# A bidirectional Mamba-2 block: an unread negation taken out, one semaphore dropped, and the engines' orders rearranged

## What is computed

```python
def reference(x, ...):
    xn = layernorm(x)
    f = mamba2(xn, forward weights)
    r = flip(mamba2(flip(xn), backward weights))
    x = x + concat(f, r) @ Wo + bo
    return x + layernorm(x) @ W.T + b + (layernorm(x) @ V_r) @ C.T

def mamba2(x, ...):
    z, xBC, dt = split(x @ Win)
    xs, B, C = split(silu(causal_conv(xBC, width 4) + convb))
    dt = softplus(dt + dtb); dA = exp(dt * A)
    h = dA[t] * h + dt[t] * B[t] * xs[t];  y[t] = C[t] @ h      # 8 heads of 64, state of 64
    y = (y + D * xs) * silu(z)
    return rmsnorm(y) * normw @ Wout
```

## Time and profile before

| | us |
|---|---|
| median of 3 runs | 636.88 |
| lowest and highest | 635.69, 637.50 |
| the profiled execution, its own time | 635.01 |
| its span, first to last instruction | 633.20 |
| TensorE busy (matmuls) | 602.9, 95% |
| ScalarE busy | 545.8, 86% |
| VectorE busy | 510.0, 81% |
| GpSimd busy | 363.1, 57% |
| granted TensorE clock, mean | 0.997 of full speed |

### The profile page before, as it was taken

One profiled execution on the slowest core, in us unless ns is written; L12 is line 12 of the kernel. 1 busy time (PEld: TensorE's weight loads), 2 busy tenths in 40 slices (PEclk: granted clock), 3 DMA queues, 4 the chain that ended last, 5 costly groups with the idle time before them and its releaser, 6 DMA issues.

```text
span 633.2 us, 13301 instructions
## 1 busy us (share of the span) xinstructions
PE 602.9 (95%) x3996; PEld 492.4 (78%) x3996; DVE 510.0 (81%) x1056; ACT 545.8 (86%) x1220; POOL 363.1 (57%) x367
## 2 busy tenths in 40 slices
PE   2998999999999999999999999999999999999995
PEld 1676788887888878887888878888788878888784
DVE  3779788986979689797888869798797978788663
ACT  4799998979997998979989799889989799897862
POOL 1026656666575664765556675656647665465933
PEclk9999999999999999999999999999999999999998
DMA  7552614245160632407132361505416071332600
GB/s 223 158 180 92 208 23 132 57 119 192 25 184 0 193 116 65 144 9 248 51 126 83 98 211 25 182 3 177 131 29 180 1 217 59 101 111 67 211 1 33
DMA packets 43544, 70.70 MB, mean 112 GB/s; under 512 B 8000, under 2 KB 30592, under 8 KB 43520
## 3 DMA queue, kind: packets, MB, share of 16 engines
q1 hardware_dynamic: 43520, 70.40, 36.5%
HBM read 59.37 MB, written 4.72 MB: 101 GB/s over the span
## 4 chain that ended last, share of the span: by engine, by line
PE 80%; ACT 9%; DVE 5%; issue 3%; POOL 2%; DMA 0%; SPq 0%; POOLq 0%; ACTq 0%; DVEq 0%
PE mi L612 17%; PE pj L485 9%; PE py L578 9%; PE pj L487 9%; PE pj L486 9%; PE py L590 6%; PE mi L565 4%; PE mi L678 3%; PE mi L545 2%; PE mi L598 2%; ACT bs L964 2%; ACT L952 1%; DVE xdt L1418 1%; POOL xw L1906 1%; PE mi L671 1%
## 5 line engine op out<-in xcount | busy, mean ns | idle before, releaser
L1406 DVE SCALAR_TENSOR_TENSOR xc<-pj,cw,xc 128x509 f32<-128x509 f32 (+2 forms) x240 | 173.9, 742 | 20.5 <-ACT xc L934 19.1
L964 ACT ACTIVATE bs<-bs,s_all 128x128 f32<-128x128 f32 x512 | 159.3, 392 | 0.0
L1929 POOL TENSOR_TENSOR yg<-yg,sz 128x512 f32<-128x512 f32 x60 | 76.6, 1287 | 87.3 <-DVE yg L1455 87.3
L485 PE MATMUL pj<-xnt_hi,w_hi 128*128 128x512 f32 x288 | 121.2, 421 | 3.8 <-DVE xnt_lo L1323 2.9
L487 PE MATMUL pj<-xnt_hi,w_lo 128*128 128x512 f32 x288 | 114.1, 396 | 0.0
L486 PE MATMUL pj<-xnt_lo,w_hi 128*128 128x512 f32 x288 | 113.9, 395 | 0.0
L612 PE MATMUL mi<-wc,yg 128*128 128x256 f32 x480 | 110.9, 384 | 0.0
L612 PEld LDWEIGHTS mi<-wc,yg 128*128 128x128 f32 x480 | 88.7, 190 | 14.0 <-issue 3.2
L1937 POOL TENSOR_TENSOR sqsum<-sqsum,sq 128x512 f32<-128x512 f32 x45 | 57.9, 1287 | 60.7 <-ACT sq L984 60.0
L1433 DVE TENSOR_TENSOR bs<-bs,gm 128x512 f32<-128x512 f32 x128 | 85.9, 676 | 6.7 <-ACT bs L970 6.3
L1906 POOL TENSOR_TENSOR xw<-xdt,w_end 128x512 f32<-128x512 f32 x48 | 49.7, 1044 | 48.7 <-DVE xdt L1418 37.5
(11 more groups left out here) (151 smaller groups left out, 1040.3 us busy)
## 6 DMA issues: line engine op xcount, KB each, us to landing
bs<-rows_dram SPq DMA_DIRECT2D x64, 512.0 KB, 5.0
es<-rows_dram SPq DMA_DIRECT2D x128, 96.0 KB, 3.3
cc<-bcm SPq DMA_DIRECT2D x32, 128.0 KB, 3.1
xres<-in_x SPq DMA_DIRECT2D x8, 512.0 KB, 3.8
out<-ot SPq DMA_DIRECT2D x32, 128.0 KB, 3.7
xin<-in_x SPq DMA_DIRECT2D x7, 512.0 KB, 4.1
cz<-bcm SPq DMA_DIRECT2D x16, 128.0 KB, 3.4
rows_dram<-s_rows SPq DMA_DIRECT2D x128, 4.0 KB
```

What stands on the lines that cost most here:

```text
L485: pe.matmul(ps[:], hi(k), xnt_hi[:, k, :], start=(k == 0), stop=False)
L964: i = nc.scalar.activation(bs[:, h, Q * c:Q * c + Q], bs[:, h, Q * c:Q * c + Q], ACT.Relu, bias=s_all[:, d, 0, c, h:h + 1], scale=-1.0)
L1406: i = dve.scalar_tensor_tensor(xc[:, t, to], pj[bank][:, of], cw[:, d, t, KW - 1 - s:KW - s], xc[:, t, to], ALU.mult, ALU.add)
L1929: pool.tensor_tensor(yg[:, d, p, :], yg[:, d, p, :], sz[:, d, p, :], ALU.mult).then_inc(yg_ready, 1)
```

## The change

`neg_s`, `s_neg` and its four calls (two in the loop, one in the first scan, one in the opening) go, and with them the semaphore `s_ready`; `bound` of head 0 waits for `wd_ready`. Besides, calls change places in the orders of SP, TensorE (in `first_scan` alone), ScalarE and VectorE; GpSimd's order changes in one place, in `forward_scan`, a `decayed_state` ahead of `mean_square`. No other instruction is added or dropped. The diff, cut to its core:

```diff
             def opening():                                   # SP
                 load_win(0, 0, 0)
+                load_small(0)
                 load_win(0, 0, 1)
-                load_small(0)
...
+                copy_c(0, 0)
                 load_win(1, 1, 0)
-                copy_c(0, 0)
...
             def turn(it, more):
+                repeat_heads(it + 1, 1, 2)
                 store("loop", it, it, 3)
-                repeat_heads(it + 1, 1, 2)
...
             def first_scan():                                # TensorE
+                b_tokens(phase, it, b, 0)
                 project(b, 0, NT - 1)
-                b_tokens(phase, it, b, 0)
...
                 intra(b, 0, 0)
+                inter(phase, it, b, 0, 0)
                 intra(b, 0, 1)
-                inter(phase, it, b, 0, 0)
...
             def bound(b, d, h):                              # ScalarE
                 if h == 0:
-                    act.wait_ge(s_ready, u + 1)
+                    act.wait_ge(wd_ready, u + 1)
...
             def reversed_scan(phase, it, b, nxt):
-                decay(b, 1, 0)
                 bound(b, 1, 1)
                 bound(b, 1, 2)
                 bound(b, 1, 3)
+                decay(b, 1, 0)
...
             def last_scan():
                 decay_w(b, 1)
+                bound(b, 1, 0)
                 square(phase, it, b, 0, 3)
                 b_tokens(phase, it, 1)
-                bound(b, 1, 0)
...
             def forward_scan(phase, it, b):
                 bound(b, 0, 0)
+                decay(b, 0, 0)
+                conv_start(b, 1, 0)
                 decay_e(b, 0)
-                decay(b, 0, 0)
                 bound(b, 0, 1)
-                conv_start(b, 1, 0)
...
+                decay(b, 0, 7)
                 square(phase, it, b, 0, 0)
-                decay(b, 0, 7)
...
                     norm1_scale(b + 1, 1)
+                    norm1_scale(b + 1, 2)
                 conv_start(b, 1, 4)
-                if ahead:
-                    norm1_scale(b + 1, 2)
                 conv_end(b, 1, 1)
+                square(phase, it, b, 0, 1)
+                square(phase, it, b, 0, 2)
                 conv_end(b, 1, 2)
                 if ahead:
                     norm1_scale(b + 1, 3)
-                square(phase, it, b, 0, 1)
-                square(phase, it, b, 0, 2)
-                gate(b, 1, 5)
                 conv_end(b, 1, 3)
                 conv_end(b, 1, 4)
+                gate(b, 1, 5)
...
             def opening():
+                norm_high("start", 0, 0)
                 split_high(0, 0, 0)
-                norm_high("start", 0, 0)
+                norm_high("start", 0, 1)
                 split_high(0, 0, 1)
-                norm_high("start", 0, 1)
...
                 conv_end(0, 0, 2)
+                gate(0, 0, 5)
                 row_copy("start", 0, 0)
...
-            def s_neg(phase, it, d):                         # VectorE
-                s_copied(phase, it, d)
-                dve.tensor_scalar(neg_s[:, d], ..., -1.0, None, ALU.mult).then_inc(s_ready, 1)
...
             def forward_scan(phase, it, b, last):
                 norm1_bn(b + 1, 0)
+                dt_value(b, 1)
...
                 feed(phase, it, last, 0)
+                conv(b, 1, 2, 3)
+                feed(phase, it, last, 1)
                 outputs(b, 0, 2)
-                feed(phase, it, last, 1)
-                conv(b, 1, 2, 3)
                 conv(b, 1, 3, 3)
                 conv(b, 1, 4, 1)
                 conv(b, 1, 4, 2)
                 feed(phase, it, last, 2)
                 conv(b, 1, 4, 3)
                 feed(phase, it, last, 3)
-                s_neg(phase, it, 1)
                 s_rest(phase, it, 1)
                 outputs(b, 0, 3)
...
             def opening():
+                conv(0, 0, 1, 3)
+                soft_one(0)
                 conv(0, 0, 2, 1)
                 split_low(0, 1, 1)
-                conv(0, 0, 1, 3)
-                soft_one(0)
```

More of the change, by code:

```diff
@@ L389, in opening @@
                 repeat_decays(0, 0, 3)
+                copy_c(0, 1)
                 put_decays(0, 1)
+                repeat_heads(0, 1, 1)
                 repeat_decays(0, 1, 0)
-                repeat_heads(0, 1, 1)
-                copy_c(0, 1)
                 repeat_decays(0, 1, 1)
@@ L1078, in first_scan @@
                 phase, it, b = "start", 0, 0
+                gate(b, 0, NT - 1)
                 b_tokens(phase, it, 0)
-                gate(b, 0, NT - 1)
                 decay_w(b, 0)
@@ L1089, in first_scan @@
                 bound(b, 0, 2)
+                decay(b, 0, 2)
                 bound(b, 0, 3)
@@ L1096, in first_scan @@
                 conv_start(b, 1, 3)
+                decay(b, 0, 4)
                 bound(b, 0, 5)
-                decay(b, 0, 4)
                 bound(b, 0, 6)
@@ L1141, in last_scan @@
                 bound(b, 1, 6)
+                bound(b, 1, 7)
                 decay(b, 1, 6)
-                bound(b, 1, 7)
                 decay(b, 1, 7)
@@ L1245, in opening @@
                 fold(4)
-                gate(0, 0, 5)
                 fold(5)
@@ L1563, in reversed_scan @@
                 mix(phase, it, b, 0, 1)
+                weights(phase, it, b, 1, 4)
                 state(phase, it, b, 1, 2)
-                weights(phase, it, b, 1, 4)
                 conv(nxt, 0, 1, 2)
@@ L1577, in reversed_scan @@
                 conv(nxt, 0, 2, 3)
+                outputs(b, 1, 0)
                 mix(phase, it, b, 0, 2)
-                outputs(b, 1, 0)
                 outputs(b, 1, 1)
                 s_copy(phase, it, 0)
+                weights(phase, it, b, 1, 6)
                 mix(phase, it, b, 0, 3)
-                weights(phase, it, b, 1, 6)
                 conv(nxt, 0, 3, 1)
@@ L1586, in reversed_scan @@
                 conv(nxt, 0, 3, 2)
-                conv(nxt, 0, 3, 3)
                 conv(nxt, 0, 4, 1)
                 conv(nxt, 0, 4, 2)
-                s_neg(phase, it, 0)
+                conv(nxt, 0, 3, 3)
                 s_rest(phase, it, 0)
@@ L1615, in first_scan @@
                 x_tokens(phase, it, 0, 3)
+                weights(phase, it, b, 0, 0)
                 s_copy(phase, it, 1)
-                weights(phase, it, b, 0, 0)
                 weights(phase, it, b, 0, 1)
+                conv(b, 1, 1, 1)
                 conv(b, 1, 0, 3)
                 state(phase, it, b, 0, 1)
-                conv(b, 1, 1, 1)
                 weights(phase, it, b, 0, 2)
@@ L1636, in first_scan @@
                 weights(phase, it, b, 0, 7)
-                s_neg(phase, it, 1)
+                conv(b, 1, 3, 2)
                 outputs(b, 0, 1)
-                conv(b, 1, 3, 2)
                 conv(b, 1, 3, 3)
@@ L1661, in last_scan @@
                 mix(phase, it, b, 0, 1)
+                state(phase, it, b, 1, 2)
                 weights(phase, it, b, 1, 2)
                 weights(phase, it, b, 1, 3)
-                state(phase, it, b, 1, 2)
                 weights(phase, it, b, 1, 4)
@@ L1671, in last_scan @@
                 outputs(b, 1, 1)
+                gate(b, 1, 1)
                 outputs(b, 1, 2)
-                gate(b, 1, 1)
                 weights(phase, it, b, 1, 6)
@@ L1703, in forward_scan @@
                     norm1_bn(b + 1, 0)
+                dt_value(b, 1)
+                if ahead:
                     norm1_bn(b + 1, 1)
                     norm1_bn(b + 1, 2)
-                dt_value(b, 1)
-                if ahead:
                     norm1_bn(b + 1, 3)
@@ L1711, in forward_scan @@
                 scores(b, 0)
+                if ahead:
+                    norm1_aggr(b + 1, 0)
                 x_tokens(phase, it, 0, 2)
                 weights(phase, it, b, 0, 0)
-                if ahead:
-                    norm1_aggr(b + 1, 0)
                 state(phase, it, b, 0, 0)
@@ L1726, in forward_scan @@
                 conv(b, 1, 0, 3)
-                conv(b, 1, 1, 2)
                 weights(phase, it, b, 0, 2)
                 dt_floor(b, 1)
+                conv(b, 1, 1, 2)
                 conv(b, 1, 1, 3)
+                if ahead:
+                    norm1_aggr(b + 1, 1)
                 weights(phase, it, b, 0, 3)
@@ L1736, in forward_scan @@
                 mix(phase, it, last, 1, 1)
-                if ahead:
-                    norm1_aggr(b + 1, 1)
                 norm2_bn(phase, it, last, 1)
@@ L1797, in opening @@
                 soft_abs("start", 0)
+                conv(0, 0, 1, 3)
+                soft_one(0)
                 conv(0, 0, 2, 1)
                 split_low(0, 1, 1)
-                conv(0, 0, 1, 3)
-                soft_one(0)
                 soft_du(0)
+                conv(0, 0, 2, 2)
                 soft_dd(0)
-                conv(0, 0, 2, 2)
                 soft_rq(0)
```

29 lines of the change are left out of this document (11 added, 18 removed).

## The result

The changed kernel takes 640.1 us in the median of six runs (638.7 to 640.35), the kernel before beside it 636.81 (635.69 to 637.5). The ratio is 1.0049, 95% interval 1.0039 to 1.006: slower, by 3.3 us or 0.5%, where I had forecast a change too small to be told from none. That is 2.4 us above my 637.7 and 0.6 above the end of my range, 639.5. The profiled execution took 640.13 us, with a span of 638.3 against 633.2.

The account below looks back on a forecast made before the run. TensorE was taken as the bound, busy 602.92 of 633.20 us. Terms -0.5 + 1.4 + 0 + 0.1 - 0.2 = +0.8 us on the median of 636.88 gave 637.7 us, range 634.3 to 639.5.

Parts of the forecast that it names:

- Negation, -0.5: Loop: without the negation the two long periods become short, 2 x 0.25 us; its waits pass to the difference `wd`.
- The bounds' new wait, 0: Reversed half of the loop: ScalarE's first bound now waits for `wd`, which comes 0.3 us ahead, so no cost.
- Rival (c): Slower: GpSimd's residual pass starts late and makes every loop period long; +2.3 us, 639.2 us, chance 0.20.
- The late conversion, 6 x 0.23: Loop: a third `norm1_scale` ahead of `conv_start(b, 1, 4)` delays project(b, 1, 7) in six periods, +1.4 us.
- Together 0: Loop: all other reorderings, permuting passes of 0.4 to 0.8 us, cost nothing in sum; bounds -0.2 x 6 and +0.1 x 6.
- Opening, +0.1: Opening: first project +0.35, TensorE's wait for the third tap -0.51, a gate ahead of a row copy +0.25.
- First scan, 0, lower bound -1.6: First scan: longest wait, 1.6 us for `yg`, hangs on VectorE's unbroken run with the same sum, so 0.
- Tail, -0.2: Tail: a bound moves ahead of a square and token copy, VectorE's third gate is no longer held up; -0.2 us.

Follow-up runs that it names:

- 3: Changed kernel with the third norm1_scale back behind conv_start(b, 1, 4) and VectorE's middle of the forward scan as before: 636.51 us, ratio 1.0008.
- 6: Kernel before with only the negation taken out, ScalarE's bounds waiting for the difference, all orders old: 636.13 us, ratio 0.9997.
- 12 to 14: Kernel before without the negation, adding in turn the opening's tap exchange, the changed last scan, the first scan's state copy exchange: 635.82, 635.51, 635.13 us.
- 1: Changed kernel with the third norm1_scale put back behind conv_start(b, 1, 4): 637.69 us, ratio 1.0018.
- 2: Changed kernel with VectorE's middle of the forward scan (taps and aggregation) as before: 636.72 us, ratio 1.0014.
- 4: Changed kernel with only VectorE's aggregation norm1_aggr(b + 1, 1) put back behind mix(1, 1): 638.05 us, ratio 1.0036.
- 5: Changed kernel with only the taps put back, so taps 2 and 3 of tile 1 are not adjacent: 637.95 us, ratio 1.002.
- 7: Changed kernel with the openings of SP, ScalarE and VectorE as before, without the negation: 640.24 us, ratio 1.0059.
- experiment 8: Changed kernel with the first scan's order of before on TensorE, ScalarE and VectorE: 638.26 us, ratio 1.0033.
- 9: Changed kernel with VectorE's dt_floor(b, 1) three places earlier in the first scan: 639.41 us, ratio 1.0054.
- 11: Changed kernel with the last scan's orders of before on ScalarE and VectorE: 639.54 us, ratio 1.0058.
- Experiment 10: Changed kernel with the first state's copy and dt_floor ahead of one aggregation and tap 2 of tile 0 in the first scan: 638.78 us, ratio 1.0035.

## Why the prediction was wrong, point by point

- **Negation, -0.5.** Right. Every kernel without it and with the loop's two late steps undone has six short periods (3, 6, 12 to 14). The difference took a wait over, but which one depends on the order: 1.17 us in 6 and 12 to 14, 2.02 in the changed kernel, and none in the periods of 1 and 3, where `wd` takes 0.18.
- **The bounds' new wait, 0.** Right, at the place and almost to the hundredth. Rival (c), that GpSimd's pass makes every period long, fell: the residual pass did start early enough.
- **The late conversion, 6 x 0.23.** Right; 1.62 in place of 1.4.
- **"Together 0" for the other moves in the loop, bounds -1.2 and +0.6.** This is the step that failed. I wrote that "the swaps among `mix`, `outputs`, `weights` and taps keep their sums up to each result that TensorE asks for". They do not: an aggregation moved from behind `mix(1, 1)` to ahead of the mixes, and I had not followed which bank TensorE's sums take. That it waited for nothing there before was no cover: it had 0.14 us. Nor did I count that two taps of one tile in a row cost more than two of different tiles. The term was 1.26, twice its upper bound, and experiments 2, 4 and 5 show both halves of it.
- **Opening, +0.1.** Right in its parts (first project 14.67 instead of 14.35, the wait for `xc` at 24.8 gone, a later wait in its place) and in the sum (7).
- **First scan, 0, lower bound -1.6.** The second failure: I gave it no upper bound, and the clock had no term at all. "An unbroken run of VectorE with the same sum" holds for `yg`, and that wait did shrink to 0.5 because TensorE came later. But within the run an aggregation went ahead of the state's copy, and `scores` went behind the second tokens, where it no longer fills VectorE's wait for them (0.22 us in the trace of after). TensorE's stretch of idleness rose from 1.0 to 1.4 us, and with that the clock fell in part of the executions. By experiment 8 this is worth 1.0 to 1.8 us in time, of which 1.10 can be seen in its place: 0.2 for the order and 0.9 for the fall. That the longer stretch brings the fall is not shown to the end (see below).
- **Tail, -0.2.** The third gate took 0.90 us instead of 1.51, as forecast. The 12 profiles with the new tail have 104.4 us from the last mark on in the mean, the four with the old one 104.7. Single ones reach from 103.7 to 105.3, so the -0.2 is neither shown nor denied.

With the two failed terms put in, the sum is -0.5 + 1.6 + 1.3 + 0.1 + 0.9 (the 0.86 of the first table) - 0.2 = +3.2 us; +3.3 was measured. The 0.86 also holds the rest of the opening and a fall of the clock that not every execution has, so the agreement is partly luck and no proof.

## What to carry to other kernels

When a list is reordered, go through it by what the bottleneck engine asks for, banks to be emptied too, and write down the margin at each: "it did not wait there before" can mean 0.14 us. Look where the small instructions go: an aggregation that takes VectorE 0.09 us from its start to the next one's costs 0.09 us in every turn when it stands ahead of such a point. And a longer pause of TensorE may cost more than its length, in the clock behind it: 0.4 us more of pause went with falls of about 0.9 us here.

## What the runs showed of the hardware

**The first slow stretch differs from execution to execution.** TensorE's first matmuls run 0.43 us apart, as in the stretch at 1.2 GHz in the first scan, and then 0.23. Here is the kernel of experiment 6, whose opening is that of before without the negation:

```profile
17.02 0.63 PE L484 MATMUL pj<-xnt_hi,w_hi 128*128 128x512 f32 x1
...
19.16 0.57 PE L486 MATMUL pj<-xnt_hi,w_lo 128*128 128x512 f32 x1
19.56 0.39 PE L504 MATMUL mi<-xnt_hi,wdt_both 128*128 128x512 f32 x1
```

Before, six matmuls took over 0.5 us; here it was 12, in the changed kernel 11, and over all 16 profiles 6 to 14. At 0.2 us each that is up to 1.6 us of chance. It is part of why the profiled execution of before was 1.8 us under its median: its first mark at 22.28 is the earliest of all, the others are at 22.66 to 24.15, 23.4 in the mean. It is also most of the +1.28 in the first row of the table. The granted clock's row says 1.00 in this stretch, so the spacing must be read, not the row. The tail goes with the same chance, whatever its order: the six profiles whose first mark is at 23.71 or later (1, 4, 5, 8, 9 and 12) have tails of 103.73 to 104.08 us, and nine of the other ten have 104.24 or more. Most of the 1.19 us of tail in experiment 8 is therefore likely to be this, and not the first scan.

The Trainium skill ("TensorE: Matmul & The Clock Gate", Part 1) says that the number of slow matmuls at a kernel's start varies from run to run; this case agrees, 6 in the kernel before against 12 in experiment 6, with the same order of the opening.

**Whether the clock falls later went with that same chance.** Eight profiles have the stretch of 1.4 us in the first scan. In the five with 11 or more slow matmuls at the start the granted share then fell to 0.5 to 0.9 (changed kernel, 1, 4, 5, 7); in the three with 8 or fewer (2, 3, 11) it stayed at 1.00. Of the seven with a stretch of 1.0 us none fell, though three had 11 to 14 slow matmuls (6, 8, 12). The one with 2.35 us fell longest. So the fall went with a longer pause and with what had gone before it. Neither was enough alone: not the pause of 1.4 us, and not the slow start. Five and three is few for such a rule, and no run changed the start on purpose. Experiment 10's profile, with 9 slow ones, lies between the two groups and decides nothing; only its times speak.

**A short VectorE instruction pays for a long GpSimd one.** So the engines do not meet at semaphores alone, as I wrote at the start. `wd`, 0.18 us, took 2.02 behind the residual pass and 1.17 behind the addition of squares; `al`, 0.18, took 1.17 behind the residual pass in experiment 9 and 0.59 behind the pass on `es` (1.0 us) in experiment 10. The Trainium skill (SBUF — State Buffer, "Who interferes with whom") names a plain `tensor_scalar`, which `al` is, among the operations that can take the pair of ports shared with GpSimd, though it reads one tile only; the two numbers of `al` agree.

**Taps of one tile next to each other.** Two that follow each other on one tile take 1.53 us, two on different tiles 1.41. I had taken order to be free there; experiment 5 puts it at 0.135 us a period.
